# A third table of blocks, and another order of work ahead of the expert loop

## The reference

```
x = x + tanh(g_xattn) * xattn(layernorm(x), ctx, mask, Wq, Wk, Wv, Wo)   # 16 heads of 64
h = layernorm(x)
shared = (silu(h @ shared_gate.T) * (h @ shared_up.T)) @ shared_down.T   # 256 wide
p = sigmoid(h @ router_w.T + routing_bias)                               # 8 experts
top 2 of p, weights = p / sum of the two
routed = sum over the two: weight * ((silu(h @ gate_w[e]) * (h @ up_w[e])) @ down_w[e])
return x + tanh(g_ffn) * (shared + routed)
```

## Time and profile before

| | |
|---|---|
| median of 3 runs | 176.14 us (175.99 to 176.2) |
| profiled execution | 176.26 us |
| its span | 174.4 us |
| PE busy | 159.9 us, 92% |
| DVE busy | 127.6 us, 73% |
| ACT busy | 111.3 us, 64% |
| POOL busy | 110.0 us, 63% |
| granted TensorE clock, mean | 0.995 |

### The profile page before, as it was taken

The page is one execution under the profiler, slowest core; times in us unless marked ns, Lnnn a source line. Parts: engine busy times, 40 slices in busy tenths (PEclk is TensorE's granted clock), DMA queues, the critical chain, the costliest instruction groups (busy, mean ns, idle before and its releaser), DMA issues.

```text
span 174.4 us, 4611 instructions
## 1 busy us (share of the span) xinstructions
PE 159.9 (92%) x1412; PEld 139.5 (80%) x1412; DVE 127.6 (73%) x612; ACT 111.3 (64%) x427; POOL 110.0 (63%) x139
## 2 busy tenths in 40 slices
PE   7799889999999999999999996997899999999970
PEld 7687669998898998898998875895677788887860
DVE  2689988665989597878597978478784777776283
ACT  3666997774868774868774968651665566665300
POOL 3675799854869744768724768567644566666621
PEclk9999999999999999999999999999999999999997
DMA  5899996730000000000000000001414223211172
GB/s 164 267 368 379 414 401 241 284 136 4 15 2 0 19 2 4 31 17 19 31 4 0 16 21 16 17 26 40 109 40 118 64 78 83 67 52 41 53 244 91
DMA packets 11096, 17.35 MB, mean 99 GB/s; under 512 B 2075, under 2 KB 6945, under 8 KB 10944
## 3 DMA queue, kind: packets, MB, share of 16 engines
q1 hardware_dynamic: 9504, 14.59, 24.3%
q0 software_dynamic: 1280, 2.20, 3.9%
q10 hardware_dynamic: 288, 0.26, 0.4%
HBM read 9.99 MB, written 7.51 MB: 100 GB/s over the span
## 4 chain that ended last, share of the span: by engine, by line
PE 47%; POOL 14%; ACT 14%; issue 12%; DMA 6%; DVE 4%; SPq 1%; DVEq 0%; POOLq 0%
ACT probs L727 8%; PE misc L411 8%; POOL ys L1449 7%; PE pt L385 5%; PE o_bank L400 5%; PE s_even L374 5%; PE proj_q L331 3%; DMA wq_raw<-wqT 3%; PE proj_k L331 3%; PE proj_k L333 3%; PE proj_k L332 3%; PE proj_q L333 2%; PE proj_q L332 2%; DMA probs<-ys 2%; POOL xs L1369 2%
## 5 line engine op out<-in xcount | busy, mean ns | idle before, releaser
L727 ACT ACTIVATE probs<-probs,negmax 128x128 f32<-128x128 f32 x128 | 49.9, 393 | 18.8 <-DVE negmax L937 18.7
L1339 POOL TENSOR_TENSOR probs<-probs,rinv 128x512 f32<-128x512 f32 x32 | 33.0, 1047 | 19.6 <-DVE rinv L951 19.5
L1449 POOL DMA_INDIRECT ys<-probsT,places x23 | 22.5, 979 | 15.0 <-ACT places L852 12.9
L727 ACT ACTIVATION_READ_ACCUMULATOR probs<-probs,negmax 128x1 f32 x128 | 24.2, 189 | 0.0
L937 DVE CUSTOM_DVE_ANT_0 probs<-s_even,mask 128x128 f32<-128x128 f32 x64 | 18.1, 283 | 5.2 <-issue 5.2
L1369 POOL DMA_INDIRECT xs<-xrow,slot x16 | 16.3, 1021 | 6.8 <-issue 3.9
L385 PE MATMUL pt<-ident_sb,probs 128*128 128x128 f32 x128 | 17.6, 277 | 1.7 <-POOL probs L1339 1.1
L374 PE MATMUL s_even<-kT,qT 64*128 64x128 f32 x128 | 18.5, 284 | 0.4 <-DVE negmax L937 0.4
L374 PE MATMUL s_odd<-kT,qT 64*128 64x128 f32 x128 | 18.5, 285 | 0.0
L374 PEld LDWEIGHTS s_even<-kT,qT 64*128 64x128 f32 x128 | 15.4, 187 | 3.5 <-issue 1.2
L937 DVE CUSTOM_DVE_ANT_0 probs<-s_odd,mask 128x128 f32<-128x128 f32 x64 | 18.1, 283 | 0.0
(11 more groups left out here) (282 smaller groups left out, 454.8 us busy)
## 6 DMA issues: line engine op xcount, KB each, us to landing
xs<-pad SPq DMA_DIRECT2D x5, 858.0 KB, 6.6
xg<-xs SPq DMA_DIRECT2D x23, 66.0 KB, 1.9
down_sb<-down SPq DMA_DIRECT2D x1, 1152.0 KB, 9.7
probs<-ys SPq DMA_DIRECT2D x4, 256.0 KB, 3.9
gu_raw<-gu SPq DMA_DIRECT2D x3, 256.0 KB, 5.8
wk_raw<-wkT SPq DMA_DIRECT2D x2, 256.0 KB, 4.0
wq_raw<-wqT SPq DMA_DIRECT2D x2, 256.0 KB, 5.0
mask<-mask SPq DMA_DIRECT2D x8, 64.0 KB, 1.9
```

Source lines behind the costliest of these rows:

```text
L727: e = act.activation(probs[:, r, l, :], probs[:, r, l, :], ACT.Exp, bias=negmax[:, r, l:l + 1], scale=-1.0, accum_out=rowsum[:, r, l:l + 1])
L1339: pool.tensor_tensor(quad, quad, rinv[:, r, 4 * u:4 * u + 4].unsqueeze(2).to_broadcast([P, 4, P]), ALU.mult).then_inc(norm_done, 1)
L1449: pool.indirect_dma_start(out=ys, out_offset=bass.IndirectOffsetOnAxis(ap=places[:, n:n + 1].bitcast(U32), axis=0), in_=y_sb[n % IN_FLIGHT ...
```

## The change

What it does, engine by engine:

- **Tables.** There are three instead of two: from the counts after batch 5 (blocks 0 to 4), after batch 6 (blocks 5 and 6), and from all (the rest). `STARTS` is [0, 5, 7], and the scatters count on three semaphores, so that blocks 5 and 6 wait for the scatters of batch 6 only. `table_steps(1)` is new work for DVE; the counts of step 3 are new products for TensorE.
- **Router copies.** `x2_raw` is doubled. The logits no longer wait for the low part. The rounded copy and the low part are made from the raw copy in SBUF instead of from the PSUM bank. The logits of the last two steps go to the bank of their own transposition instead of to a score bank.
- **Loop over pairs.** On DVE the first two norm steps of batch 2p+1 stand ahead of the score heads of group 4p+6 instead of between them, the third after the fourth head instead of after the copies; the first reciprocals come before `copy_o`. On POOL `rstd_second` comes before the scatters, of which two instead of one stand before the next multiplication. In the last turn the second half of group 14's exponentials and reciprocals move out of the loop.
- **Tail.** On TensorE `x2_transposes(2)` and `logits(2)` come before the value products of group 13; `x2_transposes(3)` and `logits(3)` come before the first and the second half of the last output projection; `ranks(3)` and the loads of two expert numbers come ahead of `x2_transposes(LAST)`; `ranks(LAST)` comes after the first block's gate and up products. ACT, DVE and POOL follow: `route_exp(2)` comes before group 15's exponentials, `x2_lo(2)` later, the weights of step 3 before the last xrow, the middle table before and after the last choice.
- **Block loop.** Shared unit 1 stands before block 7 instead of before block 5.

```diff
+STAGES = (2, 3, LAST)
+SEEN = [ROUTED[r][-1] + 1 for r in STAGES]
+STARTS = [0] + [(seen * P * TOP_K - E_ROUTED * (P - 1)) // P + 1 for seen in SEEN[:-1]]
+UNIT_AT = 2
...
@@ SP
+            for stage, start, end in zip(range(3), STARTS, STARTS[1:] + [IN_FLIGHT]):
+                sp.wait_ge(table_ready, stage + 1)
+                found = {n: find(n) for n in range(start, end)}
+                sp.wait_ge(scattered[stage], landed[stage])
+                for n in range(start, end):
+                    gather(n, found[n])
...
@@ PE, tail
             transposes(13, 1)
+            x2_transposes(2)
             scores(15, last, 3)
+            logits(2)
             values(13, last, 1)
-            x2_transposes(2)
             transposes(14, 2)
-            logits(2)
             out_project(B - 2, use)
-            transposes(15, 3, (0,))
             pe.wait_ge(ez_ready, 3)
             ranks(2)
-            transposes(15, 3, (1,))
+            transposes(15, 3)
             values(14, last, 2)
             values(15, last, 3)
+            x2_transposes(3)
             out_project_half(B - 1, use + 1, 0)
-            x2_transposes(3)
+            logits(3)
             out_project_half(B - 1, use + 1, 1)
-            logits(3)
             pe.wait_ge(gulo_ready, EXPERTS)
-            pe.wait_ge(table_ready, 1)
-            experts = {n: block_expert(n) for n in range(2)}
             pe.wait_ge(counts_read, 1)
             shared_pass(0, 0)
             shared_pass(0, 1)
-            x2_transposes(LAST)
             pe.wait_ge(ez_ready, 4)
             ranks(3)
+            pe.wait_ge(table_ready, 1)
+            experts = {n: block_expert(n) for n in range(2)}
+            x2_transposes(LAST)
...
             block_transpose(0)
             pe.wait_ge(in_down, 16)
+            block_transpose(1)
+            block_gate_up(0, experts[0])
             pe.wait_ge(ez_ready, LAST + 1)
             ranks(LAST)
-            block_transpose(1)
-            block_gate_up(0, experts[0])
             for n in range(BLOCKS):
-                if n + 2 == EARLY:
+                if n + 2 == STARTS[UNIT_AT]:
@@ ACT, tail
             copy_pt(13, 1)
+            x2_copy(2)
+            exps(14, 2, 1)
+            route_exp(2)
             exps(15, 3, 0)
-            x2_split(2)
-            exps(15, 3, 1, lambda: route_exp(2))
+            exps(15, 3, 1)
...
+            x2_hi(2)
             copy_o(14, 2)
@@ DVE, loop over pairs
-                mask_max(g + 6, p + 1, 2, islice(steps, 2))
+                run(steps, 2)
+                mask_max(g + 6, p + 1, 2, after(4, run, steps, 1))
+                recips(g + 6, 2, (0,))
                 copy_o(g + 4, 0)
-                recips(g + 6, 2, (0,))
-                run(steps, 1)
-                recips(g + 6, 2, (1,))
+                if p < PAIRS - 2:
+                    recips(g + 6, 2, (1,))
@@ DVE, table_steps(stage), the new middle one (stage 1)
+                if stage:
+                    dve.tensor_tensor(present[:], present[:], early[:], ALU.subtract).then_inc(table_step, 1)
...
+                if stage == 1:
+                    dve.tensor_tensor(early[:], early[:], full[:], ALU.add).then_inc(table_step, 1)
@@ DVE, tail
-            mask_max(15, PAIRS - 1, 3)
+            mask_max(15, PAIRS - 1, 3, after(6, recips, 14, 2, (1,)))
             copy_o(13, 1)
-            x2_lo(2)
-            recips(15, 3, (0,))
             choice = choose_steps(2)
             run(choice, 2)
+            recips(15, 3, (0,))
+            finish(choice)
             recips(15, 3, (1,))
-            finish(choice)
             finish(weight_steps(2))
             place(2)
...
+            x2_lo(2)
             x2_lo(3)
             add_attention(B - 1, use + 1)
             norm = norm2_steps(B - 1, use + 1)
             run(norm, 2)
             choice = choose_steps(3)
-            run(choice, 4)
+            run(choice, 3)
+            finish(choice)
+            finish(weight_steps(3))
             run(norm, 1)
-            finish(choice)
+            place(3)
             finish(norm)
-            finish(weight_steps(3))
             x2_lo(LAST)
-            place(3)
+            middle_table = table_steps(1)
+            run(middle_table, 3)
...
-            finish(choose_steps(LAST))
+            choice = choose_steps(LAST)
+            run(choice, 3)
             block_lo(0)
+            finish(choice)
             finish(weight_steps(LAST))
+            block_lo(1)
+            finish(middle_table)
             place(LAST)
-            block_lo(1)
-            last_table = table_steps(1)
-            run(last_table, 3)
+            last_table = table_steps(2)
+            run(last_table, 2)
             block_hidden(0)
@@ POOL, loop over pairs (p > 0) and tail
+                rstd_second(2 * p + 1)
                 if p:
-                    scatter(p - 1, 1, 2)
-                rstd_second(2 * p + 1)
+                    scatter(p - 1, 1, 3)
                 normalise(4 * p + 6, 2)
                 if p:
-                    scatter(p - 1, 2, 4)
+                    scatter(p - 1, 3, 4)
...
             scatter(2, 1, 4)
+            count_chosen(2)
             rstd_second(B - 1)
-            count_chosen(2)
             count_chosen(3)
```

More of the change, by code:

```diff
@@ L119, in build @@
         pad = sb("pad", [P, PAD_ROWS, WIDTH])
-        x2_raw = sb("x2_raw", [P, 2, P])
+        x2_raw = [sb(f"x2_raw{i}", [P, 2, P]) for i in range(2)]
         ez, den, prob = (sb(n, [P, 2, E_ROUTED]) for n in ("ez", "den", "prob"))
@@ L133, in build @@
         full, early = sb("full", [P, CANDIDATES]), sb("early", [P, CANDIDATES])
-        table_f, table = ([sb(f"{n}{i}", [P, 2], t) for i in range(2)] for n, t in (("table_f", F32), ("table", I32)))
+        table_f, table = ([sb(f"{n}{i}", [P, 2], t) for i in range(3)] for n, t in (("table_f", F32), ("table", I32)))
         xg = [sb(f"xg{i}", [P, WIDTH]) for i in range(IN_FLIGHT)]
@@ L165, in build @@
         in_down = sem("in_down")
-        scattered = [sem("scattered0"), sem("scattered1")]
+        scattered = [sem(f"scattered{i}") for i in range(3)]
         in_xg = [sem(f"in_xg{i}") for i in range(IN_FLIGHT)]
@@ L221, in build, with stage_of, table_row @@
         y_of = y_rows.rearrange("p (b k) h -> p b k h", k=TOP_K)
+        def stage_of(n):
+            return sum(n >= start for start in STARTS) - 1
+        def table_row(n):
+            stage = stage_of(n)
+            return table[stage][n - STARTS[stage]:n - STARTS[stage] + 1, :]
         def load_y(engine, n):
@@ L287, in find @@
             def find(n):
-                late = n >= EARLY
-                row = n - EARLY * late
-                return sp.value_load(table[late][row:row + 1, 0:1]).with_bounds(min_val=0, max_val=CANDIDATES)
+                return sp.value_load(table_row(n)[:, 0:1]).with_bounds(min_val=0, max_val=CANDIDATES)
             def gather(n, c):
@@ L296, in gather @@
                 sp.dma_start(xg[n % IN_FLIGHT][:], xs[bass.ds(c * P, P), :]).then_inc(in_xg[n % IN_FLIGHT], 16)
[L298 to L307, removed]
+            landed = [16 * TOP_K * (end - start) for start, end in zip([0] + SEEN, SEEN)]
+            for stage, start, end in zip(range(3), STARTS, STARTS[1:] + [IN_FLIGHT]):
[4 more added lines that the diff above has]
+                    gather(n, found[n])
             for n in range(IN_FLIGHT, BLOCKS):
@@ L591, in block_expert @@
             def block_expert(n):
[L592 to L596, removed]
+                if n in STARTS[1:]:
+                    pe.wait_ge(table_ready, stage_of(n) + 1)
+                return pe.value_load(table_row(n)[:, 1:2]).with_bounds(min_val=0, max_val=E_ROUTED)
             def stay_warm(times):
@@ L741, in copy_o, with x2_copy, x2_hi @@
                 act.copy(oT[:, r % 2, :, :].rearrange("p c q -> p (c q)"), o_of.get(g, o_bank)[:]).then_inc(ot_ready, 1)
-            def x2_split(r):
[L745 to L751, removed]
+            def x2_copy(r):
+                act.wait_ge(x2t_done, r + 1)
+                if r >= 2:
+                    act.wait_ge(lg_done, r - 1)
+                    act.wait_ge(x2lo_ready, r - 1)
+                tiles = len(ROUTED[r])
+                act.copy(x2_raw[r % 2][:, 0:tiles, :].rearrange("p t d -> p (t d)"),
+                         route_bank[r][:, P:(1 + tiles) * P]).then_inc(x2raw_ready, 1)
+            def x2_hi(r):
+                act.wait_ge(x2raw_ready, r + 1)
+                tiles, first = len(ROUTED[r]), ROUTED[r][0]
+                act.copy(xn2T_hi[:, first * P:(first + tiles) * P],
+                         x2_raw[r % 2][:, 0:tiles, :].rearrange("p t d -> p (t d)")).then_inc(x2hi_ready, 1)
+            def x2_split(r):
+                x2_copy(r)
+                x2_hi(r)
             def route_exp(r):
@@ L1074, in table_steps @@
                     dve.memset(table_f[0][:], 0.0).then_inc(table_step, 1)
-                present = exists if late else full
```

79 lines of the change are left out of this document (37 added, 42 removed).

## The result

The changed kernel took 179.11 us (median of 4 runs, 177.18 to 179.55) against 176.06 for the kernel before: a ratio of 1.016, 95% interval 1.009 to 1.023. The execution that was profiled took 177.18 us (span 175.4) at a mean granted clock of 0.997; the four others took 178.8 to 179.6 at 0.966 or 0.967. So there is about 1 us to explain in the trace, and 2 us more in most executions.

What follows compares the result with a forecast made beforehand. Block loop bound by TensorE, so the change matters through when blocks start. Loop -0.2, first hidden product 0: profiled execution 176.26 to 176.06, median 0.12 lower, 175.9 us; own range 175.6 to 176.3, whole range 174.9 to 177.0.

Steps and rivals of the forecast that it cites:

- the loop over pairs: Head-group loop before the tail: two TensorE stalls of 0.25 us shrink by 0.1 each, -0.2 us, bounds 0 and -0.5.
- the clock: Rival, chance 0.06: TensorE works little from 117.5 to 120.3, falls to 1.2 GHz; warm-ups and first blocks cost 2 us more: 178.
- the new wait: Loop over pairs: heads five to eight wait behind xrow for POOL's power step; if late, up to one scatter of 1.0 us.
- The tail: Stretch up to the last router transposition: reordered routing and output projection bring the front 1.1 us early, loop's 0.2 included.
- The last attention: Tail, after the last output projection: added at 116.45 instead of 117.95, 1.5 us early.
- the hot and weight steps of batches 4 and 5: Tail, DVE beside POOL's multiplications: two steps wait 0 to 0.7 us, taken as about half a microsecond.
- From the last attention to the last router transposition: Tail, choice, hot and weight steps all ahead of xrow: 3.3 us instead of 2.73, transposition at 119.75, 0.93 early.
- The second low part: Second block's low part, after the last router transposition: at 123.97 instead of 125.07, the front 1.1 us early.
- DVE's stretch from there to the first hidden product: Table and slot steps between the second block's low part and the first hidden product: 2.03 us, 0.93 before.
- The first hidden product: Start of block 0's hidden product: at 126.0, level with before; bounds -1.1 and +0.3 us.
- Within the loop of blocks: Last table's scan may lose a tenth or two in block 0; no wait for gathers before blocks 5 and 7.
- Slower because DVE's stretch decides: Rival, chance 0.16: DVE's steps before the first hidden product decide if the front is under 0.9 us early: 176.7.

Runs made afterwards that it cites:

- the runs with 3, 3 and 4 products: Changed kernel plus warm-up products ahead of batch 6's ranks, last router transposition, second block's transposition: ratio 1.0095; also with batch 1's norm steps back: 1.0012.

## Why the prediction was wrong, point by point

Two steps failed. The sum took the loop over pairs at -0.2 us, and it cost 0.77; with that in its place the sum of 175.9 gives 176.9, where the executions at full clock took 177.0 and 177.2. And the sum held nothing for the clock, which stood among the rivals with a chance of 0.06; it fell in eight of eleven executions, and in the one of these that was profiled it cost 2.34 us more.

*The loop over pairs* was forecast at -0.2 us, between 0 and -0.5. It cost 0.77. The step that failed is the new wait: "heads five to eight stand behind xrow, which waits for POOL's 0.57 us power step". I looked at what xrow needs and not at what runs beside it. The prediction did price a late power step, at up to one scatter of 1.0 us; that this is near what was lost is luck, since in the first turn POOL has no scatters but weight splits, and the power step was not late. DVE's and POOL's timelines of the kernel before held the price:

```profile
52.01 0.84 DVE L983 TENSOR_SCALAR xrow<-x_sb,moments,rstd 128x256 f32<-128x256 f32 x1
```

```profile
51.41 1.28 POOL L1347 TENSOR_TENSOR gu_lo<-wq_raw,gu_hi 128x512 fp32r<-128x512 f32 x1
```

The step started beside the subtraction and ended at 52.85, 0.16 after it (52.69). Moved to where the subtraction begins, it took 1.50 and ended 0.16 after it again. In the other turns the forecast was right: with the first turn undone the loop is 0.17 shorter.

The Trainium skill, "SBUF — State Buffer", section "Who interferes with whom", lists two kinds of DVE operation that can be locked out by POOL: those with two SBUF inputs, and some with one (tensor_scalar among them) in a two-port mode. I applied it to the first kind alone. The trace agrees with the second (1.50 us beside the subtraction, 0.41 without), though no run shows in which mode the step ran.

*The tail* was forecast well, measured from the loop's end. The last attention 1.3 us early (16.46 before, 15.16 after), forecast 1.5. Inside it a size was off: the hot and weight steps of batches 4 and 5 lost about 1.5 us beside POOL (1.07 and 0.86, less 0.17 and 0.22, the lengths of the same steps for one batch), not "half a microsecond". On DVE

```profile
109.67 1.07 DVE L1038 TENSOR_TENSOR hot<-rows_sb,chosen_at 128x32 bf16<-128x32 f32 x1
111.10 0.86 DVE L1053 SCALAR_TENSOR_TENSOR xrow<-top,tanh_g,share 128x4 f32<-128x4 f32 x1
...
119.37 0.17 DVE L1038 TENSOR_TENSOR hot<-rows_sb,chosen_at 128x16 bf16<-128x16 f32 x1
...
119.85 0.22 DVE L1053 SCALAR_TENSOR_TENSOR xrow<-top,tanh_g,share 128x2 f32<-128x2 f32 x1
...
124.96 0.28 DVE L1265 TENSOR_TENSOR xg_lo<-o_bank,xg_hi 128x128 fp32r<-128x128 f32 x1
...
126.79 0.41 DVE L1270 TENSOR_TENSOR kT<-kT,s_even 128x256 f32<-128x256 f32 x1
```

and on POOL

```profile
109.62 1.05 POOL L1362 TENSOR_TENSOR probs<-probs,rinv 128x512 f32<-128x512 f32 x1
110.90 1.04 POOL L1362 TENSOR_TENSOR probs<-probs,rinv 128x512 f32<-128x512 f32 x1 [0.23 <-DVE rinv L965]
```

(The two halves lie 0.23 us apart. The prediction's end of 111.05 for the second holds such a gap too: its terms, 1.0 and twice 1.04 after 107.75, give 110.83.) TensorE was busy meanwhile: its stall ahead of batch 6's router transposition is 0.30, forecast 0.4. From the last attention to the last router transposition: 3.24 us, forecast 3.3. The second low part: 0.93 early, forecast 1.1. DVE's stretch from there to the first hidden product: 1.83 us (124.96 to 126.79), forecast 2.03. The first hidden product, from the loop's end: 24.51 before, 24.49 after, forecast level. That it is this stretch, the run with part of the middle table moved showed.

*Within the loop of blocks* nothing: 31.48 us in both, no wait for a gather, the moved unit worth nothing. As forecast, but for the tenth or two that it allowed for the last table's scan.

*The clock* was the rival that decided the median. Its mechanism was right, its price too (2 us and more for the warm-ups and first blocks; 2.34 measured), and its place nearly: TensorE idles between 118.8 and 120.7 in the trace, where it was forecast to work little from 117.5 to 120.3. The chance of 0.06 was wrong. In 8 of 11 executions of the changed kernel the clock was under 0.98. I let the granted clock of 1.00 in the earlier trace rows speak for the new order, though my own working had TensorE work little in just that stretch. The Trainium skill, "TensorE: Matmul & The Clock Gate", section "Part 1: The HAM clock gate", says that idleness takes the clock back. By that rule the prediction asked for a truly idle stretch. The trace agrees that the clock falls after a stretch of little work; but TensorE had been busy 0.46 of the 2 us from 119 to 121, so the stretch was not truly idle, and the clock fell in most executions, not in all.

That the idle stretches are the cause, and not chance, the runs with added products show: with the stretches filled no profile and no execution was near 0.966, with one of them filled or fewer of them left some still fell. Why one execution falls and the next does not stays open.

*Slower because DVE's stretch decides* (0.16) named a place that does decide, but not the cause of the loss: the front, from the loop's end, came about as early as forecast (0.93 us at the second low part).

## What to carry to other kernels

Before moving a step, read what the other engine runs at the new place, turn by turn: the first turn of a loop can hold other work than the turn that was read. A stage whose waits are rearranged must be priced at both clock levels if TensorE idles more in it, and one profile is not enough to see which it gets. Warm-up products are worth their place only where they fit: three fitted a stretch of 0.83 us, and three behind two register loads cost the whole of their time (0.74).

## What the runs showed of the hardware that was not expected

The same kernel on the same chip ran at 0.997 in one execution and 0.965 in another, 2.65 us apart (176.99 and 179.64), from the same order of instructions: the fall is not certain even where it is likely. A mean clock of 0.98 can come from the first 15 us as well as from the stretch ahead of the blocks, so only the windows of a profile tell the two apart. Two register loads hold TensorE's queue 0.64 and 0.73 us in the runs with 3, 3 and 4 products, without and with the loop mended, which the views name "issue" or put down to the wait that ends beside it. The tensor_scalar norm step that took 1.50 us beside POOL's subtraction took 0.41 beside a scatter that POOL issued.
